# Nine stages and three norms stand one tick later in the plan of a four-block transformer kernel

## The chip, the cores and the metric

The kernel runs on one core of a Trainium2 chip, as one program in one launch. Time is device time in microseconds (us), the median of several executions. The core has five engines that run side by side and meet at semaphores: TensorE (PE) multiplies and transposes, VectorE (DVE) and ScalarE (ACT) read its results from PSUM and work on them, GpSimd (POOL) does work that touches SBUF alone, and SyncE (SP) issues most of the transfers. Each engine takes its instructions strictly in the order in which the program writes them.

## The reference

Four sequences of 512 tokens with 256 features go through four layers. What is computed for each sequence:

```python
# L0: transformer block, causal, 16 heads of 16
h = layernorm(x, gamma1, beta1)
attn = softmax(where(causal, Q @ K.T / 4, -inf))      # Q, K, V = h @ W + b
x1 = x + (attn @ V) @ Wo + bo
x2 = x1 + gelu(layernorm(x1, gamma2, beta2) @ W1 + b1) @ W2 + b2
x  = x + gate * (x2 - x)
# L1: adapter with one of 16 experts, chosen per sequence
hid = gelu(x @ down_W.T + down_b)
x  = layernorm((hid @ Wsel.T + bsel + domain_emb) @ up_W.T + up_b + x)
# L2: feed-forward, one of 8 experts, chosen per sequence
x  = layernorm(gelu(x @ Wi + bi) @ Wo + bo + x)
# L3: block whose norm is scaled and shifted by a timestep, attention with bias and mask
y  = ln(x) * (1 + scale) + shift
s  = where(mask, -inf, Q @ K.T / 4 + attention_bias)  # bias 4 x 16 x 512 x 512
x  = y + (softmax(s) @ V) @ Wo + bo
x  = x + gelu2(ln(x) * g2 + beta2, W1, W2)            # 256 -> 1024 -> 256
```

So each sequence has two attentions (layers 0 and 3) and three feed-forward stages (layers 0, 2 and 3), and a chain of norms between them.

## The kernel before

**Attentions set the beat.** The eight attentions run one after the other: `ATTENTIONS` lists (sequence, kind) as (0,0), (1,0), (2,0), (0,1), (3,0), (1,1), (2,1), (3,1), with kind 0 causal and kind 1 with bias and mask. Here they are called attention 0 to 7. Each has 64 units, a unit being one head by 128 queries; a unit is one *tick*. In every tick each engine does its share of the attention: PE the scores of unit U (lines 1638, 1642, 1644), the transposes of the probabilities of unit U-2 (L1659), and, every fourth tick, in those that are multiples of 4, the product of transposed probabilities and values of four units (L1673); DVE the row maximum of unit U (L1343, or L1352, which adds the bias too); ACT the exponential of unit U (L984, L987); and DVE or ACT the copy of the transposed probabilities of unit U-3 out of PSUM (L1360, L995). Every 16 ticks there are sums to be inverted, spread by a transpose (L1684), copied (L1003) and used: `normalize` (L1379) stands at ticks 7, 23, 39 and 55 of an attention, and the next values product waits for it. In a causal attention a unit has 128 keys in ticks 0 to 7, 256 in 8 to 15, 384 in 16 to 23, 512 in 24 to 31, and the same again from tick 32; in a biased one always 512.

**Beside the attentions** stands all other work, "stages" whose steps get ticks of their own. `BESIDE` (L248) is a table with one row for each attention: (tick, stage, sequence). Functions lay out a stage's steps from its first tick:

- `plan_turn`: tick t, PE transposes the tokens (L1443), all four tiles; tick t+1, ACT and DVE copy one half each to `hT` (L1011 or L1017, L1257 or L1259).
- `qkv0`, `qkv3`: turn, then `plan_qkv` from t+3: products for queries and keys (L1504) at t+3, t+4, t+9, t+10, for values (L1517) at t+5 and t+7; behind each query or key product a chain that splits the result into three bf16 parts: ACT (L1026), DVE (L1271), ACT (L1031), DVE (L1277), then transfers to DRAM.
- `block0`, `block2`, `block3`: turn, then `plan_ffn` from t+3: eight hidden products (L1546) at t+3, t+3, t+4, t+6, t+7, t+8, t+10, t+11 with gelus on ACT (L1040; ACT loads another table before and after a group of gelus), output products (L1559) at t+12 to t+15, and adding (`ff_add`, L1315 or L1317, DVE) at t+14 and t+16. `block0` goes on with the expert: turns at t+17 (L1569, L1443), products down (L1576) at t+20, expert (L1582) at t+22, up (L1587) at t+23.
- `norm(k)`: statistics on DVE at t and t+1, the inverse root on POOL from t+2 (L917 to L921), its use at t+5 (L1227), or in two steps at t+3 to t+6 (L1235, L1243). The norm with k = 1 hands the residual to POOL at t+6 (`res_l0`, L877 to L888).

`OUTPUT_AT` puts the projection of an attention's result (`project`, L1532) at ticks 8 and 9 of the next one. A turn and a `project` first wait, in `dense_banks_free`, until every result of the earlier stages has left the three PSUM banks that stages share; so they wait for `ff_add`, for the residual adds (L1301) and for the subtractions L1271.

Inside a tick the order is fixed: PE does scores, transposes, values, and then the stages' steps; DVE copy, maximum, inversion or normalising, then the stages' steps; ACT copy, exponential, spread copy, then the stages' steps. Steps of one tick stand in the order in which the table and `plan_loads` (L297) gave them. `plan_loads` puts a weight load for the next feed-forward stage on SP one tick behind the last hidden product (`w1`) and the last output product (`w2`) of the one before; transfers of the stacked queries and keys (`stack`, six of them) stand at tick 36 (in some attentions 44) and at tick 4 of the next attention.

Two rules look at the planned load of the neighbouring ticks: `copy_sides` (L363) chooses for each unit whether ACT or DVE copies its transposed probabilities, and `mask_sides` (L394) chooses for each pair of units of a biased attention whether PE adds the mask to the scores (L1642) or POOL adds it to the bias beforehand (`mask_pair`, L950), four ticks ahead. POOL also turns the mask into numbers (L939), in the same queue.

## Time and profile before

| | |
|---|---|
| median of 3 runs | 1102.37 us (1102.13 to 1111.74) |
| profiled execution, time / span | 1103.2 / 1101.4 us |
| PE busy | 993.9 us (90%), 7849 matmuls |
| PE weight loads busy | 673.5 us (61%) |
| DVE busy | 679.8 us (62%) |
| ACT busy | 681.9 us (62%) |
| POOL busy | 334.4 us (30%) |
| moved by DMA | 154.80 MB, mean 141 GB/s |
| granted TensorE clock | 0.991 of full |

Busy time is the time in which an engine executes something; waiting for semaphores is not part of it. Matmul ends are modelled, so back-to-back matmuls overlap a little in the rows. A row's idle time, in square brackets, says how long the engine had nothing to do before it, and what ended that.

### The profile page before, as it was taken

What the parts mean: (1) busy time and instruction counts of PE and PEld (TensorE: products, weight loads), DVE (VectorE), ACT (ScalarE), POOL (GpSimd) and SP (SyncE); (2) the same over time, 40 slices, a digit from 0 to 9 for tenths busy, and PEclk for the clock granted to TensorE, in tenths of its full rate; (3) what the DMA queues carried; (4) which work ended last, traced back from release to release, by engine and by line L of the source; (5) the groups of instructions that cost most, each with busy time, mean ns of one, the idle gap of its engine ahead of it and who ended that gap; (6) DMA issues with size and microseconds to landing.
All of it is one profiled execution on the core that took longest, in us unless ns stands there. A gap on an engine that the chain in (4) does not pass through costs nothing.

```text
span 1101.4 us, 22343 instructions
## 1 busy us (share of the span) xinstructions
PE 993.9 (90%) x7849; PEld 673.5 (61%) x7936; DVE 679.8 (62%) x1732; ACT 681.9 (62%) x1580; POOL 334.4 (30%) x546
## 2 busy tenths in 40 slices
PE   8878889898999899898889899899898999989898
PEld 6545557465656576566547476566576657657667
DVE  6778662737745738846672766746747764663761
ACT  4657564665675756766564756575756675665761
POOL 7401140201510661840120220730743272073101
PEclk9899999998999999999999999999999999999999
DMA  6898326033261644945625128657476478953610
GB/s 181 177 200 241 62 77 133 23 81 73 64 157 40 137 139 155 223 159 169 126 77 115 43 100 183 203 179 193 143 178 202 129 218 221 208 189 116 230 59 20
DMA packets 118385, 154.80 MB, mean 141 GB/s; under 512 B 12988, under 2 KB 80956, under 8 KB 118276
## 3 DMA queue, kind: packets, MB, share of 16 engines
q1 hardware_dynamic: 114196, 147.57, 50.1%
q0 software_dynamic: 1936, 3.97, 1.7%
q10 hardware_dynamic: 2144, 1.84, 0.5%
q8 instruction: 65, 1.06, 0.4%
q14 instruction: 44, 0.36, 0.1%
HBM read 134.47 MB, written 18.88 MB: 139 GB/s over the span
## 4 chain that ended last, share of the span: by engine, by line
PE 57%; ACT 16%; DVE 14%; issue 10%; POOL 2%; DMA 1%; another core or an unknown queue 0%; DVEq 0%; ACTq 0%; POOLq 0%
PE bank L1559 14%; PE bank L1659 9%; PE bank L1546 7%; PE bank L1673 5%; PE bank L1504 5%; PE bank L1638 4%; ACT gT L1040 3%; DVE mrow L1343 3%; ACT bias L987 3%; DVE bias L1352 2%; PE bank L1532 2%; PE bank L1517 2%; ACT L1040 2%; PE bank L1642 2%; ACT prob L984 2%
## 5 line engine op out<-in xcount | busy, mean ns | idle before, releaser
L987 ACT ACTIVATE bias<-bias,mrow 128x512 f32<-128x512 f32 x256 | 184.1, 719 | 192.9 <-DVE mrow L1352 191.0
L1352 DVE CUSTOM_DVE_ANT_0 bias<-bank,bias 128x512 f32<-128x512 f32 x256 | 175.3, 688 | 202.2 <-PE bank L1638 85.0
L984 ACT ACTIVATE prob<-bank,mrow 128x128 f32<-128x128 f32 (+3 forms) x256 | 134.8, 527 | 182.8 <-DVE mrow L1343 181.1
L1343 DVE TENSOR_REDUCE mrow<-bank 128x1 f32<-128x128 f32 (+3 forms) x256 | 124.2, 487 | 168.3 <-PE bank L1644 167.1
L917 POOL TENSOR_TENSOR norm_rows_t<-norm_rows_t,minus_half 128x4 f32<-128x4 f32 x23 | 23.8, 1033 | 617.1 <-DVE norm_rows_t L1214 617.0
L1659 PEld LDWEIGHTS bank<-ident,bias 128*128 128x128 f32 x1024 | 122.0, 141 | 103.5 <-ACT bias L987 47.7
L1659 PE MATMUL bank<-ident,bias 128*128 128x128 f32 x1024 | 156.1, 275 | 32.3 <-ACT pT L995 23.5
L1638 PE MATMUL bank<-ks,qs 128*128 128x512 bf16 (+3 forms) x425 | 143.5, 338 | 31.9 <-ACT prob L984 29.0
L1546 PE MATMUL bank<-hT,w 128*128 128x512 f32 x352 | 165.0, 596 | 0.9 <-issue 0.8
L1360 DVE COPY pT<-bank 128x512 f32<-128x512 f32 (+3 forms) x274 | 157.0, 573 | 6.9 <-PE bank L1659 5.8
L1559 PE MATMUL bank<-w,gT 128*128 128x256 f32 x704 | 160.4, 381 | 0.0
L1559 PEld LDWEIGHTS bank<-w,gT 128*128 128x128 f32 x704 | 130.3, 190 | 18.1 <-issue 2.2
L950 POOL TENSOR_TENSOR bias<-bias,negmask 128x256 f32<-128x256 f32 x192 | 127.0, 694 | 35.2 <-DMA bias<-in_fside_Bx16xSxS 32.7
L1659 PE MATMUL bank<-ident,prob 128*128 128x128 f32 x640 | 117.9, 283 | 11.7 <-ACT pT L995 6.8
L995 ACT ACTIVATE pT<-bank 128x512 f32<-128x512 f32 (+3 forms) x238 | 122.3, 514 | 0.0
L1673 PE MATMUL bank<-pT,va 128*32 128x128 f32 x3328 | 119.0, 279 | 3.4 <-DVE ctxn L1379 2.3
L1638 PEld LDWEIGHTS bank<-ks,qs 128*128 128x128 bf16 x512 | 50.1, 98 | 105.3 <-ACT prob L984 58.6
L1673 PEld LDWEIGHTS bank<-pT,va 128*32 128x32 f32 x3328 | 84.2, 110 | 25.3 <-issue 22.1
L1659 PEld LDWEIGHTS bank<-ident,prob 128*128 128x128 f32 x640 | 71.0, 145 | 34.8 <-issue 24.6
L1546 PEld LDWEIGHTS bank<-hT,w 128*128 128x128 f32 x352 | 60.8, 190 | 50.5 <-issue 50.0
L1642 PE MATMUL bank<-negmask,identb 128*128 128x512 bf16 x160 | 60.6, 379 | 5.8 <-issue 2.7
L1644 PE MATMUL bank<-causal,identb 128*128 128x128 bf16 x256 | 57.2, 224 | 2.0 <-ACT prob L984 0.6
(181 smaller groups left out, 1230.9 us busy)
## 6 DMA issues: line engine op xcount, KB each, us to landing
bias<-in_fside_Bx16xSxS SPq DMA_DIRECT2D x128, 512.0 KB, 4.4
w<-in_L_cond_W SPq DMA_DIRECT2D x16, 1024.0 KB, 5.4
qs<-q_parts SPq DMA_DIRECT2D x30, 384.0 KB, 9.7
ks<-k_parts SPq DMA_DIRECT2D x30, 384.0 KB, 11.7
q_parts<-parts SPq DMA_DIRECT2D x80, 128.0 KB
k_parts<-parts SPq DMA_DIRECT2D x48, 128.0 KB
w<-in_L_cond_Wi SPq DMA_DIRECT2D x4, 1024.0 KB, 5.3
w<-in_L_cond_Wo SPq DMA_DIRECT2D x4, 1024.0 KB, 5.7
```

The costliest lines, as they stand in the source:

```text
L950: pool.tensor_tensor(b_n, b_n, negmask[:, t, keys], ALU.add).then_inc(masked, 1)
L984: act.activation(prob_of(U), score_bank[U % 2][:, 0:n], ACT.Exp, bias=mrow[:, U % ROW_RING:U % ROW_RING + 1], accum_out=rsum[:, U % ROW_RI ...
L987: act.activation(prob_of(U), prob_of(U), ACT.Exp, scale=-1.0, bias=mrow[:, U % ROW_RING:U % ROW_RING + 1], accum_out=rsum[:, U % ROW_RING: ...
L995: act.activation(pT[:, U % PT_RING, 0:n // P, :], turn_bank[U % 2][:, 0:n].rearrange("p (k q) -> p k q", q=P), ACT.Identity).then_inc(pt_a, 1)
L1343: v.tensor_reduce(m, score_bank[U % 2][:, 0:n], AX_X, ALU.max, negate=True).then_inc(max_done, 1)
L1352: v.tensor_tensor_reduce(out=prob_of(U), in0=score_bank[U % 2][:], in1=prob_of(U), scale=-1.0, scalar=3e38, op0=ALU.add, op1=ALU.min, accu ...
L1360: v.tensor_copy(pT[:, U % PT_RING, 0:n // P, :], turn_bank[U % 2][:, 0:n].rearrange("p (k q) -> p k q", q=P)).then_inc(pt_v, 1)
L1546: mm = pe.matmul(dense_bank[FF_BANK[j]][:], w1[:, c, j * P:(j + 1) * P], hT[:, c, :], start=c == 0, stop=c == ND - 1)
L1559: mm = pe.matmul(dense_bank[FF_OUT_BANK[t // 2]][:, (t % 2) * D:(t % 2 + 1) * D], gT[:, j, t * P:(t + 1) * P], w2[:, j, :], start=j == 0, ...
L1638: mm = pe.matmul(score_bank[U % 2][:, 0:n], qs[:, hd, t * P:(t + 1) * P], ks[:, hd, 0:n], start=True, stop=l == 1 and not on_pe)
L1659: mm = pe.transpose(turn_bank[U % 2][:, k * P:(k + 1) * P], prob_of(U)[:, k * P:(k + 1) * P], ident[:])
L1673: mm = pe.matmul(ctx_bank[32 * j:32 * (j + 1), t % 2 * P:(t % 2 + 1) * P], v_h, pT[:, (GH * w + j) % PT_RING, k, :], start=e == 0 and k == ...
```

## The change

The diff touches the table `BESIDE` alone. Nine entries that are projection or feed-forward stages and three that are norms get a tick that is one higher, in attentions 1, 2, 4 and 5: the projections at 11 go to 12; block0 and block2 at 23 go to 24, block0 at 35 to 36, block2 at 55 to 56; the norms at 12 go to 13. No step is added or taken out of a stage. The norms at 48 in attentions 1 and 5, those around the block0 of attention 2, and every entry of attentions 0, 3, 6 and 7 keep their ticks.

```diff
--- before.py
+++ after.py
@@ -247,11 +247,11 @@
 STACKS_AT = [(-2, 11)] + [(-28, 4)] * 2 + [(-20, 4)] + [(-28, 4)] * 3 + [(-20, 1)]
 BESIDE = [
     [(2, norm(0), 1), (8, qkv0, 1), (24, norm(0), 2)],
-    [(11, qkv0, 2), (12, norm(1), 0), (23, block0, 0), (48, norm(3), 0), (55, block2, 0)],
-    [(8, norm(4), 0), (15, norm(5), 0), (22, norm(1), 1), (23, qkv3, 0), (35, block0, 1), (42, norm(0), 3), (60, norm(3), 1)],
+    [(12, qkv0, 2), (13, norm(1), 0), (24, block0, 0), (48, norm(3), 0), (56, block2, 0)],
+    [(8, norm(4), 0), (15, norm(5), 0), (22, norm(1), 1), (23, qkv3, 0), (36, block0, 1), (42, norm(0), 3), (60, norm(3), 1)],
     [(3, block2, 1), (20, norm(4), 1), (23, qkv0, 3), (27, norm(1), 2), (34, norm(5), 1), (36, block0, 2), (61, norm(3), 2)],
-    [(11, qkv3, 1), (12, norm(6), 0), (23, block2, 2), (40, block3, 0), (41, norm(4), 2), (48, norm(5), 2)],
-    [(11, qkv3, 2), (12, norm(1), 3), (23, block0, 3), (48, norm(3), 3), (55, block2, 3)],
+    [(12, qkv3, 1), (13, norm(6), 0), (24, block2, 2), (40, block3, 0), (41, norm(4), 2), (48, norm(5), 2)],
+    [(12, qkv3, 2), (13, norm(1), 3), (24, block0, 3), (48, norm(3), 3), (56, block2, 3)],
     [(9, norm(4), 3), (16, norm(5), 3), (23, norm(6), 1), (24, qkv3, 3), (36, block3, 1)],
     [(9, norm(6), 2), (15, block3, 2)],
 ]
```

What follows from it elsewhere in the program: `copy_sides` gives 237 copies to ACT and 275 to DVE (before 238 and 274), with 39 units on the other side than before; `mask_sides` puts the mask of 79 pairs on PE (before 80): pairs 44 and 53 (ticks 24 and 42 of attention 5) go to POOL, pair 45 goes to PE. On SP, the load of `w1` that stood ahead of a `stack` of six transfers now stands behind it, in five places.

**Place 1: PE in attention 2, ticks 34 to 36.** The names: `bank<-ks,qs` are the scores of a unit, `causal` the causal mask's product, `bank<-ident,prob` transposes of probabilities, `pT,va` the values product, `ident,h` the turn of block0. Before:

```order
L1638 MATMUL bank<-ks,qs 128x128
L1644 MATMUL bank<-causal,identb 128x128
L1659 MATMUL bank<-ident,prob 128x128
L1443 MATMUL bank<-ident,h 128x128 x8
L1638 MATMUL bank<-ks,qs 128x128
L1644 MATMUL bank<-causal,identb 128x128
L1659 MATMUL bank<-ident,prob 128x128
L1673 MATMUL bank<-pT,va 32x128 x16
```

and in the changed kernel:

```order
L1638 MATMUL bank<-ks,qs 128x128
L1644 MATMUL bank<-causal,identb 128x128
L1659 MATMUL bank<-ident,prob 128x128
L1638 MATMUL bank<-ks,qs 128x128
L1644 MATMUL bank<-causal,identb 128x128
L1659 MATMUL bank<-ident,prob 128x128
L1673 MATMUL bank<-pT,va 32x128 x16
L1443 MATMUL bank<-ident,h 128x128 x8
```

The turn went behind the attention's share of tick 36, to which a values product belongs.

**Place 2: PE behind block0 in attention 1, ticks 38 to 41.** `w,gT` is an output product of the feed-forward, `ident,exp_w` and `ident,xy` the turns of the expert stage. Before:

```order
L1559 MATMUL bank<-w,gT 128x256 x8
L1638 MATMUL bank<-ks,qs 128x128
L1644 MATMUL bank<-causal,identb 128x128
L1659 MATMUL bank<-ident,prob 128x128
L1638 MATMUL bank<-ks,qs 128x256
L1644 MATMUL bank<-causal,identb 128x128
L1659 MATMUL bank<-ident,prob 128x128
L1673 MATMUL bank<-pT,va 32x128 x4
L1569 MATMUL bank<-ident,exp_w 64x64
L1443 MATMUL bank<-ident,xy 128x128 x8
```

and in the changed kernel:

```order
L1559 MATMUL bank<-w,gT 128x256 x8
L1638 MATMUL bank<-ks,qs 128x256
L1644 MATMUL bank<-causal,identb 128x128
L1659 MATMUL bank<-ident,prob 128x128
L1673 MATMUL bank<-pT,va 32x128 x4
L1638 MATMUL bank<-ks,qs 128x256
L1644 MATMUL bank<-causal,identb 128x128
L1659 MATMUL bank<-ident,prob 128x128
L1569 MATMUL bank<-ident,exp_w 64x64
L1443 MATMUL bank<-ident,xy 128x128 x8
```

Between the last output product and the turns there are still two units' shares and a values product, but both units are now 256 keys wide; the narrow one (128 keys) went ahead of the output product.

**Place 3: DVE around tick 7 and 8 of attention 2.** `mrow` is a row maximum, `ctxn` the normalising, `xy<-bank,xy` the add of block2's result (`ff_add`), `x<-bank,x` the residual behind `project`. Before:

```order
L1343 TENSOR_REDUCE mrow<-bank 128x1
L1379 TENSOR_TENSOR ctxn<-bank,spread 128x256
L1315 TENSOR_TENSOR xy<-bank,xy 128x512
L1343 TENSOR_REDUCE mrow<-bank 128x1
L1172 BN_STATS stats<-xy 128x6 x2
L1343 TENSOR_REDUCE mrow<-bank 128x1
L1301 TENSOR_TENSOR x<-bank,x 128x512
```

and in the changed kernel:

```order
L1343 TENSOR_REDUCE mrow<-bank 128x1
L1379 TENSOR_TENSOR ctxn<-bank,spread 128x256
L1360 COPY pT<-bank 128x128
L1343 TENSOR_REDUCE mrow<-bank 128x1
L1315 TENSOR_TENSOR xy<-bank,xy 128x512
L1172 BN_STATS stats<-xy 128x6 x2
L1343 TENSOR_REDUCE mrow<-bank 128x1
L1301 TENSOR_TENSOR x<-bank,x 128x512
```

The add went behind the maximum of tick 8 and, with it, away from the normalising of tick 7; the copy of a narrow unit stands there, which ACT made before.

## Rows read from the trace of the kernel before

**Rows 1.** Page, parts 1 and 4: busy time; the chain that ended last

```profile
PE 993.9 (90%) x7849; PEld 673.5 (61%) x7936; DVE 679.8 (62%) x1732; ACT 681.9 (62%) x1580; POOL 334.4 (30%) x546
...
PE 57%; ACT 16%; DVE 14%; issue 10%; POOL 2%; DMA 1%; another core or an unknown queue 0%; DVEq 0%; ACTq 0%; POOLq 0%
```

**Rows 2.** PE's waits: line, releaser, us in total, times, longest

```profile
PE bank L1659 <- ACT pT L995: 30.3, 49, 1.6
```

**Rows 3.** Line 1638, weight loads: ns shortest/median/longest, first and last start

```profile
L1638 PEld LDWEIGHTS bank<-ks,qs x512: 95/98/152, 22.5 to 1066.9; 128*128 128x128 bf16 x171
```

**Rows 4.** Windows: length, busy PE, PEld, DVE, ACT, POOL; clock; projections

```profile
120.78:147.87 27.09, 23.35 (x179) 14.93 (x179) 20.76 (x49) 17.40 (x48) 13.31 (x19) 1.00 0.13 41
676.38:708.68 32.30, 29.96 (x262) 19.77 (x264) 23.78 (x63) 20.97 (x47) 14.81 (x23) 1.00 0.77 221
855.89:886.05 30.16, 28.86 (x258) 19.62 (x261) 22.79 (x62) 20.82 (x49) 7.18 (x13) 1.00 0.51 162
```

**Rows 5.** Windows, columns as before: three feed-forward stages

```profile
448.33:497.85 49.52, 45.81 (x317) 30.72 (x319) 29.54 (x70) 32.09 (x62) 31.13 (x46) 1.00 0.70 194
703.70:751.86 48.16, 44.88 (x316) 30.53 (x319) 25.97 (x57) 30.75 (x59) 21.87 (x33) 1.00 0.68 187
882.40:929.36 46.96, 44.66 (x315) 30.80 (x318) 24.00 (x55) 30.37 (x58) 26.30 (x38) 1.00 0.78 215
```

**Rows 6.** Timeline, (2, 35): start, length, engine, operation [idle before <-releaser]

```profile
300.34 1.07 PE L1443 MATMUL bank<-ident,h 128*128 128x128 f32 x8 [1.41 <-issue]
...
301.57 1.08 PE L1673 MATMUL bank<-pT,va 128*32 128x128 f32 x32
```

**Rows 7.** Timeline of PE, (5, 55)

```profile
782.75 0.44 PE L1443 MATMUL bank<-ident,xy 128*128 128x128 f32 x2 [0.66 <-DVE xy L1243]
783.56 0.44 PE L1443 MATMUL bank<-ident,xy 128*128 128x128 f32 x2 [0.38 <-DVE xy L1243]
```

**Rows 8.** Timeline of DVE, (2, 7)

```profile
254.84 0.41 DVE L1379 TENSOR_TENSOR ctxn<-bank,spread 128x256 f32<-128x256 f32 x1
...
255.17 0.68 DVE L1315 TENSOR_TENSOR xy<-bank,xy 128x512 f32<-128x512 f32 x1
```

**Rows 9.** Windows: two ticks behind a feed-forward's last product

```profile
188.53:191.69 3.16, 2.32 (x25) 1.67 (x24) 1.90 (x5) 1.13 (x5) 0.00 (x0) 1.00 0.36 67
751.86:756.29 4.43, 3.76 (x52) 2.93 (x51) 3.69 (x8) 1.91 (x4) 0.00 (x0) 1.00 0.82 211
929.36:932.11 2.75, 2.70 (x45) 2.12 (x45) 1.54 (x4) 1.28 (x3) 0.00 (x0) 1.00 0.43 87
```

**Rows 10.** Windows: expert stages, (3, 54) to (3, 61), (5, 41) to (5, 48)

```profile
501.79:516.84 15.05, 12.92 (x119) 8.02 (x119) 9.39 (x24) 10.80 (x23) 0.00 (x0) 1.00 0.46 151
756.29:769.30 13.01, 11.83 (x88) 7.26 (x88) 8.02 (x21) 10.25 (x21) 0.00 (x0) 1.00 0.63 212
```

**Rows 11.** Page, part 5: the mask's product on PE; busy, mean ns

```profile
L1642 PE MATMUL bank<-negmask,identb 128*128 128x512 bf16 x160 | 60.6, 379 | 5.8 <-issue 2.7
```

**Rows 12.** Timeline of POOL and DVE, (5, 17) to (5, 24)

```profile
694.74 3.69 POOL L877 TENSOR_TENSOR x<-x,xy 128x256 f32<-128x256 f32 x4 [8.98 <-DVE h L1227]
...
698.51 2.78 POOL L880 TENSOR_TENSOR x<-x,b 128x256 f32<-128x256 f32 x4
...
701.38 1.78 POOL L939 TENSOR_SCALAR negmask<-maskraw 128x256 bf16<-128x256 uint8 x2
...
704.11 2.56 POOL L950 TENSOR_TENSOR bias<-bias,negmask 128x256 f32<-128x256 f32 x4
...
707.45 0.69 DVE L1352 CUSTOM_DVE_ANT_0 bias<-bank,bias 128x512 f32<-128x512 f32 x1 [0.20 <-PE bank L1642]
```

**Rows 13.** Windows around a fall of the granted clock in attention 2

```profile
257.30:264.00 6.70, 5.48 (x41) 3.66 (x39) 5.63 (x18) 3.22 (x12) 2.03 (x5) 1.00 0.30 104
264.00:270.90 6.90, 6.42 (x40) 3.34 (x39) 6.73 (x23) 4.73 (x17) 1.49 (x3) 0.51 0.00 1
270.90:276.00 5.10, 4.53 (x42) 2.48 (x42) 5.10 (x14) 4.29 (x13) 0.64 (x3) 1.00 0.00 0
```


## The prediction, made before the changed kernel was run

> **What bounds the kernel now.** I read the shares and the chain of waits first. TensorE (PE) is busy for 993.9 us of a span of 1101.4, and the chain that ended last is 57% PE, 16% ScalarE (ACT), 14% VectorE (DVE) [rows 1]. So a time can only move through what PE does (it does almost the same work in both kernels) or through its gaps, 107.5 us in all. The list of waits says what these gaps are: short, many, and at handovers inside the attentions; the largest group is 30.3 us for 49 waits on ACT's copy, none over 1.6 us [rows 2]. There is no long stall for the change to remove.
>
> Then I laid the plan over the trace. Tick t of attention a, written (a, t), begins with the weight load of its scores product. There are exactly 512 of these, one for each unit, so the n-th in order of time is unit n [rows 3]. The stretches named below run from one of these loads to another, and **PE's gaps in a stretch are its length less PE's busy time**.
>
> What a tick costs depends on its neighbours. If a stage's product stands in it, PE is the limit and DVE and ACT wait. If not, the tick goes at the pace of maximum, exponential and copy, and PE has small gaps. A move by one tick keeps both the stages' work and the distances inside a stage. It changes only what stands at fixed ticks: the values product (every 4th tick, a multiple of 4), normalising (ticks 7, 23, 39, 55), the width of an unbiased unit (128 keys in ticks 0 to 7, 256 in 8 to 15, and so on), the projection at tick 8, and the stages that did not move. The moved stages began at 11, 23, 35 and 55, one before a multiple of 4, and now begin on it. The kernel before already has stages of both kinds, and that gives most of my prices.
>
> **The parts.**
>
> *Three projections, 11 to 12.* The biased one in attention 5 has gaps of 32.30 - 29.96 = 2.34 us over 14 ticks from its turn. The same stage beginning on a multiple of 4, (6, 24), has 30.16 - 28.86 = 1.30 [rows 4]. That is 1.0 us less. The two in attentions 1 and 4 lie beside unbiased units and have more to lose (27.09 - 23.35 = 3.74), but no stage on a multiple of 4 stands beside such widths. Their bounds are 0 and 1.0 us; I take 0.5 each, since the project products at 8 and 9 keep their place and an attention tick of its own (tick 11) now stands behind them. Sum -2.0 (0 to -3.0).
>
> *Three feed-forward stages, 23 to 24.* From turn to last product the biased one at (5, 23) has gaps of 48.16 - 44.88 = 3.28 us. Those at tick 36 have 46.96 - 44.66 = 2.30 and 49.52 - 45.81 = 3.71, the latter with two norms beside it [rows 5]. So -1.0 to +0.4 each. I take -0.3, the middle: sum -0.9 (-3.0 to +1.2).
>
> *Attention 2, 35 to 36.* The turn at tick 35 waits 1.41 us for DVE's two subtractions of the projection ahead. In the new order the scores of tick 36 and its values product, 1.08 us, are ahead of it [rows 6], while the subtractions stay at tick 34. The gap is filled: -1.0 (0 to -1.4).
>
> *Feed-forward stages, 55 to 56.* In attention 5 the turn stops twice, for 0.66 and 0.38 us, for the norm's last step, which stays at ticks 53 and 54 [rows 7]. One tick (with its values product) later that is over: -1.0 (0 to -1.0). In attention 1 there is no such wait: 0.
>
> *The end of a stage.* After the last product DVE goes: maximum, normalising (0.41 us), adding the feed-forward's result (0.68 us), and then PE may go on [rows 8]. Normalising stays at tick 39, the add goes to 40. So DVE normalises while PE still multiplies. Two ticks behind the last product have gaps of 3.16 - 2.32 = 0.84 and 4.43 - 3.76 = 0.67 us in stages that began at 23, and 2.75 - 2.70 = 0.05 in one that began at 36 [rows 9]. That is -0.8 and -0.6 in attentions 1 and 5. In three places the next stage was not moved: the projects of (2, 8) and (6, 8) and the turn of (4, 40) now stand in the very tick of the add that they wait for. The tick between, which PE used as filler, now lies ahead of the last product. Filler of one narrow or one biased tick is lost: 0.2, 0.4 and 0.2 us. Sum of the five -0.6 (-1.4 to +0.8).
>
> *The expert stage behind three of them.* Its products go from 43, 45, 46 to 44, 46, 47 (in attention 2 from 55, 57, 58 to 56, 58, 59): the values product of tick 44 (56) now stands ahead of the first, and not between the first and second, where PE waits for a gelu between two table loads. Seven ticks here have gaps of 13.01 - 11.83 = 1.18 us in the old position and 15.05 - 12.92 = 2.13 in the new [rows 10]: +0.95 at most, part of it by a late DVE at that place. I take +0.6 each: +1.8 (0 to +2.9).
>
> *Mask terms.* The planner's rule puts 79 pairs' mask on PE, not 80: two products fewer [rows 11]. One shows as 0.379 us, but its neighbour starts before it ends, so I count 0.2 us each, between nothing and the full figure: -0.4 (0 to -0.8). GpSimd (POOL) gets a pair more, number 44, which serves ticks 24 and 25 of attention 5. POOL adds the residual (3.69 + 2.78 us), loads the mask (1.78), then adds the first pair (2.56, to 706.67) [rows 12]. The residual waits for the norm, now a tick later, about 1.0 us: pair 44 is ready at 707.7. Before, DVE took tick 24's maximum at 707.45 [rows 12]; without the turn ahead of it, it would come at about 707.0. A wait of 0.7 us appears (0 to 2.0).
>
> *At no price:* copies of transposed probabilities (one goes from ACT to DVE; both have 38% free), and the weight loads for later stages, which SP now issues behind six stack transfers in the same tick: they are wanted some 20 ticks later, in the tightest place, (4, 43), seven ticks. Without that cover a transfer's whole landing would show.
>
> **The sum:** -2.0 - 0.9 - 1.0 - 1.0 - 0.6 + 1.8 - 0.4 + 0.7 = -3.4 us against the profiled execution's 1103.2, so 1099.8. That execution is 0.8 us above the median of 1102.37; beside medians I expect **1099 us**.
>
> **Rivals.**
>
> *The gaps only move: 1102 us.* A gap of PE is the end of a chain over three engines. Work put into one gap is missing in the next: the values product that fills the turn's wait at 23 is no longer there at 24 to 26. For it: both pairs of stages compared above differ in their neighbours too. Against it: the ends of stages, 0.05 against 0.7, differ just where normalising left the chain. Only the mask products count: 1103.2 - 0.4 - 0.8 = 1102.0. The Trainium skill (Perfetto Trace Analysis, Identifying the Most-Contended Engine) says that busy time of matmuls is no good measure for TensorE and that weight-load time should be used; that is 61% here [rows 1], by which the 90% is no bound and small gaps are not time to be won: this rival's result.
>
> *Slower: 1106 us.* The values product is on the wrong side. Everything behind a gelu waits for two table loads, and a stage on a multiple of 4 has the values product ahead of this wait. Price by the unfavourable rows: six feed-forward stages at +0.4 are 2.4, three experts at +0.95 are 2.9, ends -1.4, masks -0.4, POOL +0.7: +4.2, so 1103.2 + 4.2 - 0.8 = 1106.6, some 1106. It decides if the projections win nothing (less than 1 us in all) and the stage at (3, 36), not that at (6, 36), is the pattern.
>
> *All favourable ends: 1094 us.* -3.0 - 3.0 - 1.4 - 1.0 - 1.4 + 0 - 0.4 + 0 = -10.2; with half of the surplus, since they hardly come together, about -8.
>
> *The clock.* The granted clock stood at 0.51 of full, the 1.2 GHz level, from 264.0 to 270.9 us, and PE had been busy 5.48 of the 6.70 us before it fell [rows 13]. 40 matmuls took 6.90 us there, against 42 in 5.10 at 2.4 GHz behind it [rows 13]: one such stretch more or fewer is up to 2.0 us. The stretch lies behind (2, 8), a place that the change touches. The Trainium skill (TensorE: Matmul & The Clock Gate, What's actually happening) says that the half clock is the default and activity releases it; the trace's fall after a stretch 82% busy agrees with that poorly, and I price by rows alone.
>
> **The numbers.** Chances: the forecast (1097 to 1101) 0.42; gaps only move 0.27; slower 0.16; favourable ends 0.10; the clock, to either side, 0.05. The range runs from the favourable ends nearly to the sum of the unfavourable bounds: 1093 to 1107 us. About 1% (11 us) is what a measurement of this kernel can tell from no change. Below 1091.3 lies only the full favourable sum with a clock stretch less: 0.05. Above 1113.4 needs something not in my list: 0.03. Within: 0.92.
>
> **What would show it.** In the changed profile: gaps of about 1.3 us over the 14 ticks from (5, 12); hardly a wait ahead of the turn at (2, 36) and at (5, 56); gaps under 0.3 us in the two ticks behind the last product, in (1, 40) and (5, 40), but 0.7 to 0.9 in (2, 8) and (4, 40); a wait of DVE for a masked pair at (5, 24); PE's busy time lower by under 1 us. I am wrong if the gaps between the expert's products grow by over 1 us each, if the projections keep their gaps, or if the clock falls in other places.

## The result, and the profile after

| | before | changed |
|---|---|---|
| median | 1104.12 us (1100.01 to 1111.74, 21 runs) | 1110.43 us (1105.46 to 1115.7, 21 runs) |
| profiled execution, time / span | 1103.2 / 1101.4 us | 1108.96 / 1107.1 us |
| mean granted clock, profiled | 0.991 | 0.988 |
| mean granted clock, all runs | 0.9909 (145 runs beside the experiments) | 0.9872 (21 runs) |

The ratio is 1.0054, 95% interval [1.0041, 1.0068]: **6 us slower**, where I had forecast 3 us faster and a range up to 1107. It is within the 1% that a measurement can tell from no change, to which I gave 0.92, but the interval leaves the sign in no doubt. Two executions in the slower state that a chip sometimes shows, one of g4 (1300.67 us) and one of the kernel before (2958.01 us), are left out of every ratio here. The page of the changed kernel, parts 1 and 4, against [rows 1]:

```profile
PE 999.1 (90%) x7846; PEld 678.5 (61%) x7934; DVE 679.4 (61%) x1733; ACT 680.9 (62%) x1579; POOL 335.8 (30%) x550
...
PE 59%; ACT 16%; DVE 13%; issue 10%; POOL 1%; another core or an unknown queue 0%; DVEq 0%; ACTq 0%; POOLq 0%
```

The shares say nothing of the loss. PE is busy 5.2 us longer with 3 recorded matmuls fewer, which points to a lower clock. But busy time of PE is a rough measure here. The plan has 7936 matmuls before and 7934 after; both of these traces lack 87 or 88 of them, and in the complete trace of h2 PE is busy for 1002.9 us. A matmul that was not recorded counts as a gap, so the prediction's 107.5 us of gaps are some 8 too many (h2 has 100.0 in 1102.9), and gaps of windows are good to some tenths of a us. The largest wait of PE grew by 4.1 us and three occurrences against [rows 2]:

```profile
PE bank L1659 <- ACT pT L995: 34.4, 52, 1.8
```

The windows that answer to [rows 4, 5, 9, 10], with their columns (length; busy PE, PEld, DVE, ACT, POOL; clock; DMA share; GB/s). They are, in this order: the projections of attentions 1 and 5, 14 ticks from the turn; block0 of attention 5, turn to last product; the two ticks behind the last product in attentions 1 and 5; the expert stage of attention 5, seven ticks.

```profile
120.89:145.90 25.01, 23.07 (x177) 14.95 (x179) 19.46 (x48) 16.31 (x46) 11.92 (x17) 1.00 0.14 44
681.73:713.62 31.89, 29.28 (x259) 19.58 (x262) 23.15 (x62) 19.72 (x46) 13.23 (x21) 1.00 0.77 214
709.10:758.72 49.62, 45.19 (x315) 30.60 (x317) 26.47 (x58) 30.70 (x58) 24.66 (x38) 1.00 0.74 200
186.51:189.40 2.89, 2.35 (x24) 1.62 (x23) 1.71 (x4) 1.30 (x5) 0.00 (x0) 1.00 0.17 40
758.72:762.94 4.22, 3.76 (x52) 2.86 (x52) 3.36 (x7) 1.92 (x4) 0.00 (x0) 1.00 0.56 162
762.94:777.71 14.77, 12.91 (x119) 8.01 (x119) 9.10 (x23) 10.59 (x22) 0.00 (x0) 1.00 0.56 193
```

The projection of attention 1 has gaps of 1.94 us (3.74 before: 1.8 less, where I took 0.5). That of attention 5 has 2.61 (2.34 before, 1.30 expected). Block0 has 4.43 (3.28 before, 3.0 expected). Behind the last product there are 0.54 and 0.46 us (0.84 and 0.67 before, 0.04 and 0.07 expected); in the two ticks from (2, 8) and from (4, 40), where I expected 0.7 to 0.9, there are 0.83 and 0.80. The expert stage has 1.86 (1.18 before, 1.8 expected).

### The profile page after: what moved, and what is told of

It is laid out like the page before. It is cut to its first block, busy times and chain, and to the rows that moved or that the text cites. A ratio compares the mean times of both kernels' runs of the same rounds, so it can differ in the third digit from the quotient of the medians.

```text
span 1107.1 us, 22344 instructions
## 1 busy us (share of the span) xinstructions
PE 999.1 (90%) x7846; PEld 678.5 (61%) x7934; DVE 679.4 (61%) x1733; ACT 680.9 (62%) x1579; POOL 335.8 (30%) x550
## 4 chain that ended last, share of the span: by engine, by line
PE 59%; ACT 16%; DVE 13%; issue 10%; POOL 1%; another core or an unknown queue 0%; DVEq 0%; ACTq 0%; POOLq 0%
PE bank L1559 14%; PE bank L1659 9%; PE bank L1546 8%; PE bank L1673 6%; PE bank L1504 5%; PE bank L1638 4%; DVE bias L1352 3%; ACT bias L987 3%; ACT gT L1040 3%; DVE mrow L1343 2%; PE bank L1532 2%; PE bank L1517 2%; ACT L1040 2%; PE bank L1642 2%; ACT prob L984 2%
## 5 line engine op out<-in xcount | busy, mean ns | idle before, releaser
L950 POOL TENSOR_TENSOR bias<-bias,negmask 128x256 f32<-128x256 f32 x196 | 129.6, 693 | 39.9 <-DMA bias<-in_fside_Bx16xSxS 37.4
```

The source lines that it names most:

```text
L950: pool.tensor_tensor(b_n, b_n, negmask[:, t, keys], ALU.add).then_inc(masked, 1)
```

## Where the time went

Windows that begin at a turn hide what the turn did to the ticks ahead of it. So from here I compare **times between ticks that have the same work behind them in both kernels**: the start of tick 20, of 40, of (2, 8). From (1, 8) to (5, 40) this works well: a stretch that no edit touches, and in which the clock stays up, repeats there within 0.05 us from one kernel's trace to another's (0.15 behind (4, 8), where a half-clock stretch has just ended). Behind (5, 40) it works less well. Untouched stretches differ by up to 0.35 us ((5, 50) to (5, 52), (6, 8) to (6, 16)), and (7, 8) to (7, 18) by 2.4 us, with the clock at full; in that stretch DVE waits 2.1 us for a transfer of the bias in the kernel before and not at all in g2. So 0.3 us more or less in the last row below mean nothing, and attention 7 is left out. Four kernels moved the row of one attention each, so their neighbours were those of before.

| stretch | forecast | found, clock aside | read in |
|---|---|---|---|
| attention 1, (1, 8) to (1, 20): projection | -0.5 | -1.0 | e1 |
| attention 4, (4, 8) to (4, 20): projection | -0.5 | -1.3 | e3 |
| attention 5, (5, 8) to (5, 20): projection | -1.0 | +0.9 | e4 |
| ticks 20 to 40 of attentions 1, 4 (to 41), 5, POOL among them | 0.0 | -0.2, +0.3, +0.8 | e1, e3, e4 |
| attention 1, (1, 40) to (2, 24): end, expert, stage at 56 | 0 | +1.9 | e1 |
| attention 2, (2, 34) to (3, 8): stage at 36, expert | -0.4 | +0.9 | g3 |
| attention 5, (5, 40) to (6, 24): end, expert, stage at 56 | -0.6 | +1.5 | e4 |
| sum | -3.0 | +3.7 | |

(The forecast's fourth entry is -0.9 for the stages at 24, +0.2 for (4, 40) and +0.7 for POOL; its mask products, -0.4, come on top.) The rest goes with the clock. Over the 145 runs of the kernel before, a mean clock lower by 0.001 went with 0.77 us more; the changed kernel's 21 runs were lower by 0.0037, which makes 2.8 us. 3.7 + 2.8 = 6.5, against 6.1 between the means (1110.5 and 1104.4 us). By their means the four kernels with one row moved lie 1.3, 1.2, -1.1 and 1.6 us over the kernel before, 2.9 in all and not 6.1. Some 2 us of the difference go with the clock: theirs is lower than that of the kernel before by 0.0012 in sum, that of the four rows together by 0.0037.

**What the clock does** is seen in one window, (1, 47) to (2, 8), first in the changed kernel, then in e1, where the same instructions stand at the same ticks:

```profile
196.99:256.60 59.61, 54.99 (x375) 37.06 (x379) 28.25 (x68) 32.95 (x79) 7.72 (x13) 0.91 0.27 54
```

```profile
197.91:254.77 56.86, 50.88 (x374) 33.98 (x378) 28.09 (x68) 32.98 (x79) 7.72 (x13) 1.00 0.28 57
```

PE is busy 4.1 us longer at a mean of 0.91 and the stretch takes 2.75 us more. But the half-clock stretches near (1, 47) and (1, 52) are there too in the traces of e2, e3 and g2, where attention 1 was as before or had only its projection moved. A further one, behind (2, 63) in the changed kernel, is the first of these rows, at 0.50 of full, the 1.2 GHz level; PE had been busy for 3.94 of the 5.50 us before it. It too stands in other traces, in e2's and in h5's, and h5 moves no stage:

```profile
365.50:368.90 3.40, 3.31 (x37) 2.34 (x38) 2.67 (x6) 2.89 (x7) 3.14 (x8) 0.50 0.00 0
360.00:365.50 5.50, 3.94 (x46) 2.44 (x44) 5.30 (x15) 3.36 (x9) 1.28 (x2) 1.00 0.01 0
```

What such a stretch costs depends on the work it meets. (2, 8) to (2, 24), the place of [rows 13], takes the same time in the kernel before, which has 6.9 us at half clock there, and in e2, which has none:

```profile
254.43:276.82 22.39, 19.49 (x145) 11.97 (x143) 20.59 (x60) 14.42 (x49) 4.16 (x10) 0.85 0.15 49
```

```profile
258.23:280.62 22.39, 17.75 (x146) 10.83 (x144) 20.59 (x60) 14.39 (x49) 4.16 (x10) 1.00 0.16 48
```

DVE is busy for 20.59 of the 22.39 us in both, and PE's longer work (19.49 for 17.75 us) did not lengthen the stretch. A stretch as long at (1, 47) costs 2.5 us ((1, 46) to (1, 52) takes 11.49 us in h2 and 8.97 before), and the 3.4 us at half clock behind (2, 63) cost 2.1 ((2, 34) to (3, 8) takes 83.53 us in the changed kernel and 81.43 in g3, where the same stages stand at the same ticks and the clock stays up).

## Experiments

Eighteen kernels in five groups, each group on a chip of its own (e; f; g; h; k). Each ratio is against runs of the kernel before on the same chip, with its 95% interval. Where a kernel is set beside the changed kernel, that one was measured on another chip.

**One row of the table at a time** (e1 to e4: the changed row of attention 1, 2, 4 or 5, the others as before).

```diff
-    [(11, qkv3, 1), (12, norm(6), 0), (23, block2, 2), (40, block3, 0), (41, norm(4), 2), (48, norm(5), 2)],
+    [(12, qkv3, 1), (13, norm(6), 0), (24, block2, 2), (40, block3, 0), (41, norm(4), 2), (48, norm(5), 2)],
```

> Only the row of attention 1 is moved (projection 11 to 12, norm 12 to 13, block0 23 to 24, block2 55 to 56); rows 2, 4 and 5 stay. Theory A (clock): the changed kernel's trace reaches the up product of attention 1 2.1 us ahead of before and its next turn 2.7 us behind, and the clock is at half in between (two stretches between 198 and 212 us) where before it is full; the values product that no longer stands between the products down and expert leaves PE thin there. Expects 3 to 4 us over before, with half-clock stretches between (1, 45) and (1, 56). Theory B (local gaps alone): up to the up product the row gains 1 us, and the last part costs one wider unit, 0.4 us: 0.5 us under before, no half-clock stretch that before has not. Theory C (POOL and mask sides): nothing here touches them, so 0.

> Only block0 of attention 2 is moved, 35 to 36. Theory A (clock): 1 us of the changed kernel's loss at this place is a half-clock stretch at the start of attention 3; expects 3 us over before with that stretch, 2 without. Theory B (local gaps): the changed trace loses 2.0 us from the turn of (2, 36) to the turn at (3, 3), since the turn starts one attention tick later and nothing is won back before the norm that stays: 2 us over before whatever the clock. Theory of the prediction: 1 us under before.

> Only the row of attention 4 is moved (projection 11 to 12, norm 12 to 13, block2 23 to 24). It is the row of attention 1 without the expert stage and without the stage at 55. Theory A (clock) and theory B (local gaps) both expect 0.8 us under before, and no new half-clock stretch. A loss of over 1 us here would speak against both.

> Only the row of attention 5 is moved; with it go the three pairs whose mask changes sides. Theory C (POOL and masks): DVE waits for the masked pair at (5, 24), 0.7 us as predicted, up to 2. Theory B (local gaps): the changed trace loses 3.0 us from the projects of (5, 8) to those of (6, 8): 0.9 up to the end of the projection, 1.3 at the turn and the first hidden product, 0.8 at the end. Expects 3 us over before, and the clock full throughout. Theory A alone (all of the loss is clock) expects 0.

Measured: e1 1106.22 us, ratio 1.0021 [1.0, 1.0043]; e2 1105.71, 1.0008 [0.9989, 1.0028]; e3 1103.72, 0.999 [0.997, 1.0011]; e4 1106.17, 1.0009 [0.999, 1.0028]. No row carries the loss alone, and the ratios are too near 1 to rank the rows. The traces rank them (table above): attention 4 wins 1.0, attention 5 loses 3.1, both as the theory of local gaps expected. Attention 1 loses 0.7, where that theory expected a gain of 0.5, and attention 2 loses 0.9 without its half-clock stretch, where it expected 2.

**The mask's side** (f3: e4, with pairs 44, 45 and 53 as before).

```diff
+ON_PE[44:46], ON_PE[53] = [True, False], True
```

> The row of attention 5 moved, but the three pairs of units keep their side of the mask (44 on PE, 45 on POOL, 53 on PE). Theory C (POOL): in the run with the row alone DVE waited 0.93 us for POOL at (5, 24), and PE's gap at (5, 26) was 1.85 us. Without pair 44 on POOL this wait is gone: the row costs 2 us where it cost 3.1, less 0.4 us for two mask products more. Theory D alone: the gap at (5, 26) stays above 1.5 us.

Measured: 1108.36 us, 1.0047 [1.003, 1.0064], no gain in the median, at a mean clock of 0.9887; a half-clock stretch at (5, 52) stands in its trace. In the stretch that matters, (5, 20) to (5, 40), it does win. First e4, then f3; the kernel before takes 57.29:

```profile
696.52:754.57 58.05, 53.47 (x378) 35.55 (x382) 31.71 (x72) 36.41 (x72) 32.78 (x47) 1.00 0.69 184
```

```profile
699.12:756.14 57.02, 53.28 (x378) 35.56 (x382) 31.62 (x72) 36.42 (x72) 30.34 (x43) 1.00 0.69 190
```

The difference is 1.03 us. In e4 POOL ends pair 44 at 708.69 and DVE, ready 0.93 us earlier, starts on it then (POOL, then DVE, (5, 24)):

```profile
706.13 2.56 POOL L950 TENSOR_TENSOR bias<-bias,negmask 128x256 f32<-128x256 f32 x4
```

```profile
708.72 0.69 DVE L1352 CUSTOM_DVE_ANT_0 bias<-bank,bias 128x512 f32<-128x512 f32 x1 [0.93 <-POOL bias L950]
```

**Clock and values product** (f1, f2: `VALUES_AT = 9` in the changed kernel and in the one before; f4: the kernel before with 3 to 8 spare transposes per tick in thin stretches).

```diff
-VALUES_AT = 8
+VALUES_AT = 9
```

```diff
+def filler(n, k):
+    for _ in range(n):
+        pe.transpose(dense_bank[k][:, 0:P], ident[:], ident[:])
```

> The changed kernel with every values product one tick later (VALUES_AT 9 for 8), so that the moved stages meet it again where they met it before: between a turn and its first hidden product. Theory D (the values product is PE's filler while hT is copied; moved ahead of the turn it fills nothing, the three ticks behind the turn lose it): the gaps that grew, 0.5 us at (1, 25) to (1, 27), 1.4 at (1, 55) to (1, 59), 0.7 at (5, 55) to (5, 59) and those of attention 5, shrink again; expects 3 us or more under the changed kernel, at most 2 over before. Theory E (a later start alone costs, whatever lies in between): expects no gain against the changed kernel, so 5 to 6 over before.

> The control: the kernel before with VALUES_AT 9. A values product stays between a turn at 23 and its first hidden product at 26 (at 25 for 24), but now meets the hidden product of tick 29. Theory D: within 1.5 us of before, either way. If a later values product were good by itself, this would gain as much as the same edit in the changed kernel (theory E): then 3 us under before.

> The kernel before with idle transposes (3 in a tick, 8 between the products expert and up) into a free PSUM bank, in the thin stretches: behind the four expert stages, in ticks 10 to 22 of attention 2 and at the start of attention 4. They compute nothing. Theory A (the granted clock): where a trace has half-clock stretches in (1, 46) to (1, 55) they cost 3.5 us, and some runs have them and others don't; with the fillers none is left behind tick 40 of attention 1, and the median falls by 1 to 3 us and the spread of the runs from 10 us to about 6. If the clock costs nothing that counts: 0 to 2 us over before, what the transposes themselves take.

Measured: f1 1108.03 us, 1.0049 [1.0029, 1.007]; f2 1102.48, 0.9989 [0.9978, 1.0001]; f4 1105.74, 1.0018 [1.0006, 1.003], at a mean clock of 0.9966. By their means a later values product takes 1.6 us off both kernels (f1 beside the changed kernel), which for f2 is not clear of noise. So it isn't what tells them apart: f1 stays 5 us behind the kernel before, where my theory allowed 2. From (7, 8) to the end both traces take 3.7 to 3.8 us more than before, with one half-clock stretch in each. f4 holds the clock, and its runs spread over 3.4 us only, against 6.1 beside it; but the transposes take more than they give back. This filler, at least, does not win the clock's part.

**Side of the values product, and the two halves of the change** (g1: turn ahead of the values product within five of the ticks; g2: only projections and norms moved, and with them the mask of pair 44 to POOL; g3: only feed-forward stages; g4: g2 with nine ticks for the values product in attentions 0 to 5).

```diff
+                if U in TURN_FIRST:
+                    for step, args in steps.get(U, []):
+                        do[step](*args)
                 V = U - VALUES_AT
```

> The changed kernel, but in ticks 24 and 56 of attentions 1 and 5 and in tick 24 of attention 4 PE makes the feed-forward's turn ahead of the values product of the same tick, not behind it. So the values product stands again between the turn and the first hidden product. Theory 'filler' (the values product covered what DVE and ACT need from the turn to the first hidden product; in the changed kernel PE has 0.5 to 1.9 us more gaps in the 8 ticks from each of these turns): about 0.7 us less in each of the five places, 3 to 4 us less than the changed kernel, so about 1106 to 1107 beside a kernel before at 1104. Theory 'clock' (more stretches at half clock, whatever the order): as the changed kernel, 1110. Theory 'distance' (it is the later start beside the norms and subtractions that costs, not the values product's side): as the changed kernel, 1110, with the gaps of ticks 24 to 32 of attention 5 still near 3.9 us against 1.9 before.

> The kernel before, with the three projections at 12 and the three norms at 13 alone; all feed-forward stages keep their ticks. Theory 'two halves' (the projections won more than forecast and the feed-forward stages lost more): PE's gaps from tick 8 to the turn at 23 shrink by 1.8 us in attention 1, 2.0 in attention 4 and 0.5 in attention 5, as in the changed kernel, and behind that nothing is lost: about 3 us faster than before, 1101 us, ratio 0.996 to 0.998. Rival 'it only moves': the projections' last subtractions now meet the turn at 23, and the 2 to 3 us come back as a wait there: 1104 us, ratio 1.000. Theory 'clock': also 1104, with two thirds of any difference in the granted clock.

> The changed kernel, with the three projections back at 11 and the three norms at 12; the six feed-forward stages stay one tick later. Theory 'two halves': what the projections won is gone and what the feed-forward stages lose is left: 8 to 10 us slower than before, 1112 to 1114 us, ratio 1.007 to 1.009. Rival 'it only moves' (the parts are not additive: what the projections won is won by the later turn behind them as well): as the changed kernel, 1110, ratio 1.0054 or less. Theory 'clock': anything between 1104 and 1110, with a mean granted clock lower by 0.003 than the kernel before.

> The kernel before with the projections at 12 and the norms at 13, and in attentions 0 to 5 the values product nine ticks behind the first of its four units, not eight (in attentions 6 and 7 eight, where nine cost 1.6 and 4.2 us in the kernel before). In ticks 12, 24 and so on it stands then at 13, 25, always one tick behind a turn that begins on 11, 23 or 55 by one more, between turn and first product. If the gains add: nine was 4.0 us ahead at the end of attention 5 in the kernel before, the projections 2 to 3: about 1098 to 1100 us, ratio 0.994 to 0.996. If they are the same gain, taken twice: 1100 to 1102.

Measured: g1 1109.82 us, 1.0044 [1.0024, 1.0064]; g2 1104.46, 1.0002 [0.9983, 1.002]; g3 1107.65, 1.0034 [1.0014, 1.0053]; g4 1103.43, 0.9995 [0.9975, 1.0015]. g1 ends my theory that the values product has to lie between turn and first product: (1, 20) to (1, 40) takes 52.77 us, against 51.41 in the changed kernel. g2 wins 1.0 us up to (1, 20) and gives 0.9 back by (1, 40): "it only moves" holds for it, and "two halves" is wrong. g3 loses 0.9 us around (2, 36) with the clock at full, so the stage itself costs there. g4 stayed above both of its ranges.

**Apart or in one tick** (h1: the changed kernel, values product one tick later in the nine ticks with a moved turn; h5: the kernel before, values product of tick 12 at tick 11, with the turn, in attentions 1, 4, 5; h2: apart in seven ticks where before had them together; h3: the norms at 48 moved to 49).

```diff
+LATE_VALUES = (64 + 12, 64 + 24, 64 + 56, 128 + 36, 256 + 12, 256 + 24, 320 + 12, 320 + 24, 320 + 56)
...
-                if 0 <= V < ALL_UNITS and V % GH == 0:
+                if 0 <= V < ALL_UNITS and V % GH == 0 and U not in LATE_VALUES:
                     values(V // GH)
+                if U - 1 in LATE_VALUES:
+                    values((V - 1) // GH)
```

> The changed kernel, but in the nine ticks to which a turn was moved ((1,12), (1,24), (1,56), (2,36), (4,12), (4,24), (5,12), (5,24), (5,56)) the values product is made one tick later. Nothing else moves, no stage and no other values product. Theory 'two in one tick' (a turn of 1.09 us and a values product of 1.08 us behind each other in one tick keep the next scores from PE's queue, DVE starves and is late in the next ticks, where PE then waits): DVE's idle time ahead of the maximum of (5,13), 2.06 us in the changed attention 5, falls to about 1.2, the gap of 0.96 us at (5,15) goes, about 0.4 to 0.9 us are won in each of the biased places and 0.2 to 0.5 in the others: 2.5 to 4 us less than the changed kernel, 1106.5 to 1108 beside a kernel before at 1104. Theory 'distance' (what counts is how many ticks with work for DVE lie between turn and first product, and which filler they have is indifferent): less than 1 us won, 1109.5 to 1110.5. Theory 'clock': no difference beyond that in the mean granted clock.

> The kernel before, with the values product of tick 12 made at tick 11 in attentions 1, 4 and 5, where it stands ahead of the projection's turn. No stage moves. Theory 'two in one tick': attention 5 reaches tick 20 later by 0.6 to 1.1 us against the kernel before (the projection at 12 costs 0.86 there), with an idle time of DVE near 2 us behind the pair. Theory 'distance': within 0.2 us of the kernel before at (5,20). Read from the trace alone, since stretches that no edit touches repeat to 0.02 us.

> The kernel before, with the values product one tick later at the seven ticks where it meets a turn in that kernel: (1,40), (2,52), (3,36), (4,40), (5,40), (6,24), (6,36). Theory 'two in one tick': 0.3 to 0.9 us won in each, 2 to 4 us in all, 1100.5 to 1102, ratio 0.996 to 0.998. Theory 'distance' and theory 'clock': no difference, 1104, ratio within 0.9995 to 1.0005.

> The changed kernel, with the two norms that feed the feed-forward stages at 56 moved one tick later too (48 to 49 in attentions 1 and 5), as the other norms of the moved stages were. Theory 'late norm' (the norm's last two steps, 1.80 and 1.72 us on DVE, hold up the maxima of ticks 54 and 55; before, the turn at 55 lay in that wait, now nothing does; there are 1.2 to 1.8 us more from tick 47 of attentions 1 and 5 to tick 8 of the next): with the norm's steps at 54 and 55 the turn at 56 lies in the wait again, 1 us is won in each place, 1108. Theory 'two in one tick': the values product and the turn stay together at 56, so less than 0.5 us each: 1109.5 to 1110.5.

Measured: **h1 1103.79 us, ratio 1.0001 [0.9983, 1.0019]**, no stage moved back; h2 1105.8, 1.0012 [0.9993, 1.0032]; h3 1109.14, 1.0049 [1.003, 1.0069]; h5, one execution, 1107.6.

By their means h1 is 6.3 us faster than the changed kernel (1104.2 and 1110.5), more than the 2.5 to 4 expected. Stretches with the same state of the clock in both traces give 0.38 us at (1, 12), 0.83 at (1, 56), 0.16 at (2, 36), 0.27 at (4, 12), 1.15 at (5, 12) and 0.96 at (5, 56) (beside g3 at (2, 36) and f3 at (5, 56), which have those stages at the same ticks): 3.8 us in all. Its mean clock is 0.9895, against 0.9872, which by the slope above makes 1.8 more; why the clock rose is not shown. (1, 56) to (2, 8), first in the changed kernel, then in h1:

```profile
212.97:256.60 43.63, 41.17 (x291) 27.96 (x295) 17.39 (x40) 24.66 (x53) 5.54 (x8) 1.00 0.36 73
```

```profile
212.54:255.34 42.80, 41.58 (x293) 27.95 (x294) 17.39 (x40) 24.66 (x53) 5.56 (x8) 1.00 0.36 74
```

The mechanism shows at (5, 12). The changed kernel: PE, then DVE, each row a start, a length, the instruction and the idle time before it.

```profile
683.60 1.08 PE L1673 MATMUL bank<-pT,va 128*32 128x128 f32 x32
684.61 1.09 PE L1443 MATMUL bank<-ident,xy 128*128 128x128 f32 x8
685.76 0.38 PE L1642 MATMUL bank<-negmask,identb 128*128 128x512 bf16 x1
...
688.84 0.63 PE L1659 MATMUL bank<-ident,bias 128*128 128x128 f32 x4 [0.96 <-ACT pT L995]
```

```profile
686.18 0.69 DVE L1352 CUSTOM_DVE_ANT_0 bias<-bank,bias 128x512 f32<-128x512 f32 x1 [2.06 <-PE bank L1642]
686.79 0.08 DVE L1352 DVE_READ_ACCUMULATOR2_ANT mrow<- 128x1 f32 x1
686.79 0.69 DVE L1257 COPY hT<-bank 128x512 f32<-128x512 f32 x1
687.40 0.74 DVE L1172 BATCH_NORM_STATS2 stats<-x 128x6 f32<-128x256 f32 x2
688.05 0.67 DVE L1352 CUSTOM_DVE_ANT_0 bias<-bank,bias 128x512 f32<-128x512 f32 x1
```

Values product and turn, 2.1 us together, stand ahead of the next unit's mask product. DVE has nothing for 2.06 us (1.22 in the kernel before). Then it has the maximum, the copy of the turned tokens and the norm's statistics one behind the other, the next maximum is late, and PE waits 0.96 us at (5, 15). In h1 (its lines are one higher) the turn stands alone and the values product a tick later; DVE starves for 0.91 us, then

```profile
680.93 0.69 DVE L1353 CUSTOM_DVE_ANT_0 bias<-bank,bias 128x512 f32<-128x512 f32 x1 [0.91 <-PE bank L1643]
```

and PE's gap at (5, 15) is gone. (5, 8) to (5, 20) in e4, in h1 and in h5, against 26.23 before:

```profile
669.43:696.52 27.09, 25.36 (x215) 18.32 (x217) 17.94 (x51) 16.23 (x40) 1.82 (x5) 1.00 0.84 211
```

```profile
669.49:695.42 25.93, 25.32 (x218) 18.23 (x217) 18.02 (x51) 16.22 (x40) 1.82 (x5) 1.00 0.98 224
```

```profile
674.48:701.19 26.71, 25.64 (x219) 18.35 (x217) 17.57 (x51) 15.99 (x39) 2.40 (x6) 1.00 0.85 214
```

Apart, the later projection wins 0.30; together it loses 0.86; together without a move loses 0.48, with DVE idle for 1.71 us and a gap of 1.07 behind it. Both directions are shown at this one place. The rule has its limits. The joining in h5 costs nothing in attentions 1 and 4 (0.00 and 0.04 us by tick 20), and h1 wins nothing in ticks 20 to 40 of any attention (the differences to the changed kernel are 0.01 us in attentions 1 and 5). Of h2's seven places one wins, (6, 24); its first four ticks take 0.49 us less, first before, then h2:

```profile
855.89:864.10 8.21, 7.24 (x69) 4.85 (x69) 7.51 (x24) 6.18 (x17) 1.84 (x5) 1.00 0.54 175
```

```profile
857.34:865.06 7.72, 7.11 (x71) 4.88 (x70) 7.42 (x24) 6.38 (x17) 1.83 (x5) 1.00 0.56 189
```

At (5, 40) 0.4 us are lost, and at the other five nothing changes. What distinguishes the places was not tested.

h3 shows the other half in attention 1. With the norm at 48, left behind by an expert stage that ends a tick later, DVE does the expert's last add and the statistics without a break, with maxima between them (e1, DVE):

```profile
201.73 0.68 DVE L1334 TENSOR_TENSOR xy<-bank,xy 128x512 f32<-128x512 f32 x1
202.44 0.75 DVE L1172 BATCH_NORM_STATS2 stats<-xy 128x6 f32<-128x256 f32 x2
203.11 0.54 DVE L1343 TENSOR_REDUCE mrow<-bank 128x1 f32<-128x384 f32 x1
```

(1, 47) to (2, 8) takes 56.86 us in e1. In h3, also at full clock, it takes 1.75 less:

```profile
199.07:254.18 55.11, 51.62 (x378) 34.00 (x379) 27.68 (x68) 33.16 (x79) 7.73 (x13) 1.00 0.28 58
```

In attention 5 it is worth 0.4 us. The means show less than these 2.1 us: 1109.5 for h3 and 1110.5 for the changed kernel, at clocks of 0.9880 and 0.9872. Where the rest went is not shown. The planner also gave eight copies of attentions 1 and 5 another side in h3, so the norm's share is not isolated.

**All mended, and six stages alone** (k1: h1 with h3's norms, f3's masks and block0 of attention 2 at 35; k2: only the stages at 11 and 23 and the norms at 12 of attentions 1, 4 and 5 moved, apart from the values products, masks kept).

```diff
-    [(11, qkv0, 2), (12, norm(1), 0), (23, block0, 0), (48, norm(3), 0), (55, block2, 0)],
+    [(12, qkv0, 2), (13, norm(1), 0), (24, block0, 0), (48, norm(3), 0), (55, block2, 0)],
```

> The changed kernel with every suspected cost taken out at once: values products one tick behind the moved turns, the norms that feed the stages at 56 at 49, block0 of attention 2 back at 35, and the masks of pairs 44, 45 and 53 on the sides of the kernel before. If the causes are these and add, with the stretches as they stood in the single runs (attention 1 -1.6 to tick 40 and 0 behind it, attention 2 0, attention 4 -1.3, attention 5 -0.3 to tick 20, -0.2 to tick 40, 0 behind it), the traces' local difference to the kernel before is -3 us and the median 1101 to 1102, ratio 0.997 to 0.998. If the masks or the norms only moved their cost, 1103 to 1105.

> The kernel before with only the projections at 12 and the feed-forward stages at 24 (norms at 13), the values products of those six ticks one tick later, and the masks on their sides of before. The stages at 35 and 55 keep their ticks. By the same stretches: -1.6 (attention 1, to tick 40), -1.3 (attention 4), -0.5 (attention 5), sum -3.4 and nothing behind it: 1101 us, ratio 0.996 to 0.998. If the block at 55 behind an expert stage one tick later loses what the earlier part won (as the parts of the first runs did not add), 1104.

Measured: k1 1102.38 us, 0.9988 [0.9966, 1.001]; **k2 1101.13 us, 0.9977 [0.9957, 0.9998]**, faster than the kernel before by 2.5 us, with an interval that only just leaves out no change (0.2 to 4.7 us), in the best of eighteen kernels. The stretches are firmer, and came as expected (-1.6, -1.3, -0.5): (1, 8) to (1, 40) and (4, 8) to (4, 41) of k2,

```profile
115.49:187.29 71.80, 67.31 (x468) 44.87 (x469) 39.74 (x92) 42.73 (x104) 15.60 (x21) 1.00 0.36 81
530.10:604.76 74.66, 69.56 (x486) 46.25 (x487) 40.56 (x92) 43.17 (x108) 9.16 (x13) 0.99 0.43 98
```

against 73.37 and 75.94 in the kernel before, and 82.97 against 83.52 for (5, 8) to (5, 40). But behind it something is lost, against the expectation: (5, 40) to (6, 8) takes 0.60 us more than before, with the clock at full. So a later start does win at these places, and what it meets there, or behind it, can take the gain away.

## Why the prediction was wrong

**The step that failed** is the premise of the parts: that a piece of PE's work put next to a wait fills it, and that a stage on a multiple of 4 is priced by another stage on a multiple of 4. It gave -1.0 at (5, 12), -1.0 at (2, 36), -1.0 at (5, 56) and 0 at (1, 56). Found were +0.9, +0.9 (with the expert stage, for which +0.6 stood), +1.3 up to (6, 8) (end and expert stage together forecast at 0) and +1.9 (end, expert stage and project together forecast at 0). At (5, 12) PE has the next scores behind the filler, and DVE, which PE waits for a tick or two later, starves in the meantime. I had read the pair of a values product and a turn as a gap filled; there it is a gap handed to DVE and got back. At (1, 56) and (5, 56) the pair costs 0.83 and 0.96 us (h1), and with the norms at 49 the ticks from 47 or 40 on take 1.75 and 0.4 less (h3). At (2, 36) the pair costs 0.16 us only; the wait itself had another cause than I took, as told below.

Point by point:

- *Projections.* Unbiased: right in direction and too small, -1.0 and -1.3 for -0.5 each. Biased: wrong in sign. My row for it, (6, 24), has both products in one tick too and gaps of 1.30 only [rows 4]; h2 shows that parting them there wins 0.49 us. So the row held a cost of the pair that I did not see, and at (5, 12), with the norm's statistics beside it, the pair costs 1.15. It was the wrong neighbour.
- *Stages at 24.* Nearly right. With the masks on their sides (f3) ticks 20 to 40 of attention 5 take 0.27 us less than before, and in attention 1 they take 0.17 less, where I took 0.3; attention 4 loses 0.27 by tick 41, where -0.1 stood. The window from turn to last product says otherwise (4.43 us of gaps for 3.28), since it begins at the moved turn.
- *The turn at 36 no longer waits.* It does not, but the attention does. PE behind (2, 35) in the changed kernel:

```profile
302.00 0.23 PE L1638 MATMUL bank<-ks,qs 128*128 128x128 bf16 x1 [0.67 <-ACT prob L984]
...
302.93 0.30 PE L1659 MATMUL bank<-ident,prob 128*128 128x128 f32 x1 [0.64 <-issue]
303.17 1.08 PE L1673 MATMUL bank<-pT,va 128*32 128x128 f32 x32
304.18 1.09 PE L1443 MATMUL bank<-ident,h 128*128 128x128 f32 x8
```

  The 1.41 us of [rows 6] came from DVE being behind with two subtractions; scores and exponentials need DVE as much as the turn does. 0.67 + 0.64 = 1.31 of it stays, and 0.3 us more comes behind the turn. By (2, 52), behind the stage, 0.48 us are lost, and 0.40 more by (3, 8), behind the expert stage.
- *The turn at 56.* I left the norm at 48 and called its wait over. The steps of 1.7 to 1.8 us still delay the maxima of 54 and 55, and the turn that used to lie in that time is gone from it (changed kernel, (5, 55)):

```profile
789.99 0.63 PE L1659 MATMUL bank<-ident,bias 128*128 128x128 f32 x4 [1.09 <-ACT pT L995]
```

- *Ends of stages.* Right in direction, a third of the size: 0.30 and 0.21 us less for 0.8 and 0.6. *Expert stages:* right, gaps of 1.86 for 1.8 in attention 5. Together the two came near their forecast: (1, 40) to (1, 52) 0.0 us for -0.2 (e1), (5, 40) to (5, 48) +0.15 for 0.0 (e4). So what attentions 1 and 5 lost behind tick 40 they lost at the stages at 56.
- *Masks.* POOL's wait was forecast at 0.7 and measured 1.0.
- *Copies, at no price.* I counted the net, one copy from ACT to DVE. In fact 39 of the 512 change sides. h1 moves no copy against the changed kernel, so its gain has nothing to do with them; but no kernel moved the stages and kept the copies, so their share in the other stretches is open. The weight loads did cost nothing: in the changed trace PE waits for none of them.
- *Clock.* Half of the loss, nearly. I had allowed a chance of 0.05 and 2.0 us for one stretch; it is 2.8 us in the mean of 21 runs, and the very stretch of [rows 13] costs nothing where it lies. That part has no single cause: mean clocks were 0.9893, 0.9901, 0.9910 and 0.9921 with one row moved each, 0.9906 with the projections moved alone (g2) and 0.9921 with the feed-forward stages alone (g3), against 0.9909 before. Whether the order of the changed kernel brings its clock down, or how, stays open.
- *The range.* Its upper end, 1107 us, was 2 below the sum of my own unfavourable bounds (+1.2, +0.8, +2.9 and +2.0, the others 0: 1109.3 us), and the bounds themselves ended at 0 for the places that lost most.
- *The rivals.* The one that was slower named the values product's side and 1106.6; the sign was right. It took the ends of stages at their favourable -1.4; with my unfavourable +0.8 it would have said 1108.8. Its places were not right: the stages at 24 cost 0.9 in all, POOL's wait included, and g1 refutes the side. The Trainium skill (Perfetto Trace Analysis, Identifying the Most-Contended Engine) judges how close TensorE is to its peak by its weight loads, among others, and not by its matmuls' busy time. That small gaps are therefore no time to be won was my own reading of it; weight loads are 61% in both pages and in h1's, which took 3.8 us of gaps out.

## What to carry to other kernels

Before moving work in a kernel whose engines hand each other one unit at a time, ask for each new pair of neighbours on the bounding engine how long the next engine gets nothing, and what that engine then has queued. At (5, 12) 2.06 us without work for DVE came back as a gap of 0.96 us in PE two to three ticks later; at other places the same pair cost nothing, so each place wants its own look at the trace. Price a move between points that have equal work behind them in both orders, not from the moved step on. When a stage moves, move what feeds it and check who else now meets its end.

## What the runs showed of the hardware

- Stretches without an edit and at full clock repeat within 0.05 us across traces of different kernels in most of the kernel ((1, 8) to (5, 40)), while whole executions of one kernel spread over 10 us. About half of the variance of the 145 runs goes with the mean granted clock (correlation -0.71), at 0.77 us per 0.001.
- A stretch of 6.9 us at half clock cost 0.0 us where DVE was busy for 20.59 of 22.39 us, and 2.5 us at another place.
- Keeping PE busy with spare transposes held a mean clock of 0.9966 over 12 runs, against 0.991, and made the kernel 2 us slower all the same.
